# Router logits of two mixture-of-experts layers: gate columns as weights, tokens moving in two column halves

## The reference, cut to what matters

```python
# layer 0, x_flat: 625 x 1024, gate_w: 1024 x 8
router_logits = x_flat @ gate_w
router_probs = jax.nn.softmax(router_logits, axis=-1)
top_k_probs, top_k_idx = jax.lax.top_k(router_probs, 2)
...
# layer 1, xt: 625 x 1024, gate_w: 16 x 1024
scores = jax.nn.softmax((xt @ gate_w.T).astype(jnp.float32), axis=-1)
top_w, top_i = jax.lax.top_k(scores, 2)
```

## Time and profile of the kernel before

| | us |
|---|---|
| median of 3 runs | 1849.68 (1846.18 to 1851.08) |
| the profiled execution | 1855.41 |
| its span, first to last instruction | 1853.6 |
| PE busy in it | 1773.3 (96%) |
| DVE, ACT, POOL busy | 743.3, 404.6, 644.7 |
| mean granted PE clock | 0.976 |

### The profile page before, as it was taken

One profiled execution on the slowest core, in us unless ns is written; L12 is line 12 of the kernel. 1 busy time (PEld: TensorE's weight loads), 2 busy tenths in 40 slices (PEclk: granted clock), 3 DMA queues, 4 the chain that ended last, 5 costly groups with the idle time before them and its releaser, 6 DMA issues. The chain is left out here.

```text
span 1853.6 us, 21767 instructions
## 1 busy us (share of the span) xinstructions
PE 1773.3 (96%) x8374; PEld 1118.6 (60%) x8374; DVE 743.3 (40%) x1528; ACT 404.6 (22%) x744; POOL 644.7 (35%) x539
## 2 busy tenths in 40 slices
PE   9999999998999999999999999999999999999963
PEld 5475446444545777556677765577654776676641
DVE  5885003233525222454355557530621222222227
ACT  1000000002411011001576757411000322222223
POOL 0657872120000186777888620000300222222220
PEclk9999999998999999999899999999999999999987
DMA  9663124271620144333222136060411799999943
GB/s 352 185 180 83 2 47 114 64 226 27 268 84 5 37 127 130 97 97 85 54 56 54 41 86 176 33 254 12 138 63 46 295 413 409 406 410 407 404 165 109
DMA packets 104468, 289.08 MB, mean 156 GB/s; under 512 B 61942, under 2 KB 69336, under 8 KB 91611
## 3 DMA queue, kind: packets, MB, share of 16 engines
q1 hardware_dynamic: 29033, 224.83, 32.7%
q0 software_dynamic: 68160, 51.85, 12.5%
q10 hardware_dynamic: 7198, 11.36, 2.0%
HBM read 257.19 MB, written 30.32 MB: 155 GB/s over the span
## 5 line engine op out<-in xcount | busy, mean ns | idle before, releaser
L609 POOL DMA_INDIRECT table_d<-wring x85 | 173.7, 2044 | 108.6 <-issue 68.9
L381 PE MATMUL bank<-wring,region_a 128*125 128x512 f32 x480 | 207.6, 593 | 1.6 <-DVE region_a L755 0.7
L972 POOL DMA_INDIRECT wring<-xl_d,wring x85 | 108.9, 1282 | 257.8 <-DMA xr_d<-flat_b 231.9
L381 PEld LDWEIGHTS bank<-wring,region_a 128*125 128x125 f32 x480 | 89.6, 188 | 115.3 <-issue 113.9
L2292 PEld LDWEIGHTS bank<-picked_t,wring 128*128 128x128 f32 x1280 | 145.3, 194 | 7.6 <-issue 7.3
L2292 PE MATMUL bank<-picked_t,wring 128*128 128x128 f32 x1280 | 147.2, 278 | 0.1
L397 PE MATMUL bank<-flat_d,wring 128*128 128x312 f32 (+1 forms) x512 | 135.0, 426 | 0.0
L985 POOL DMA_INDIRECT score_d<-wring x85 | 110.7, 1302 | 68.3 <-DMA score_d<-wring 46.1
L972 POOL DMA_INDIRECT wring<-xr_d,wring x85 | 111.1, 1307 | 25.9 <-issue 24.4
L397 PEld LDWEIGHTS bank<-flat_d,wring 128*128 128x128 f32 x512 | 96.7, 189 | 37.9
L2307 PE MATMUL bank<-wring,unit_t 128*128 128x512 f32 x160 | 74.0, 605 | 0.0
(11 more groups left out here) (432 smaller groups left out, 2740.0 us busy)
## 6 DMA issues: line engine op xcount, KB each, us to landing
wring<-in_experts SPq DMA_DIRECT2D x60, 2048.0 KB, 12.8
wring<-in_L_Ws SPq DMA_DIRECT2D x6, 2048.0 KB, 27.0
table_d<-eq_buf SPq DMA_DIRECT2D x2, 3072.0 KB, 28.2
score_d<-no_edge SPq DMA_DIRECT2D x2, 3072.0 KB, 32.5
wring<-table_d POOLq DMA_DIRECT2D x10, 610.4 KB, 7.3
wring<-score_d SPq DMA_DIRECT2D x5, 1093.8 KB
wring<-pid_d ACTq DMA_DIRECT2D x17, 312.5 KB, 4.1
wring<-in_edge_w ACTq DMA_DIRECT2D x17, 312.5 KB, 5.2
```

What stands on the lines that cost most here:

```text
L381: ins = pe.matmul(bank[0:R, :], act_t[:, k, tok(t)], w[:, k * HALF:(k + 1) * HALF], start=(k == 0), stop=(k == chunks - 1))
L609: pool.indirect_dma_start(out=tables_d[b % 2], out_offset=bass.IndirectOffsetOnAxis(ap=edge_at[:, b:b + 1], axis=0), in_=edge_sums[:, b, : ...
L972: pool.indirect_dma_start(out=to[:, g % 2, j, :], out_offset=None, in_=table, in_offset=bass.IndirectOffsetOnAxis(ap=index[:, b:b + 1], ax ...
```

## The change

The roles of the two operands are exchanged. The gate columns become the weights (128 partitions by 64 columns, SMALL = 64) and the turned tokens move through them. Of the five tiles the even ones (0, 2, 4: 375 columns) give partitions 0 to 63 of the bank, the odd ones (1, 3: 250 columns) give partitions 64 to 127; the two alternate within each chunk, 16 matmuls for a router. The result has the gate columns on the partitions, so it is turned back: DVE copies both halves from PSUM to SBUF (`dve_keep_logits`; in layer 0 to new room in a weight slot, in layer 1 to `hid_sq`, which is free then), and PE makes three transposes into a second `dring` bank (`pe_turn_logits`). In layer 0 they stand after the fourth of the eight matmuls of half 0, tile 3; in layer 1 behind the first piece of L1932. In layer 1 PE now waits for all five turned tiles before the first matmul. `dve_top2` reads the second bank, with rows 64 columns apart.

```diff
-        def pe_logits(pe, act_t, gate, ne, before=None):
+        def pe_logits(pe, act_t, gate, ne):
             bank = dring.produce(pe)
-            for t in range(T):
-                if before:
-                    before(t)
-                for k in range(K):
-                    ins = pe.matmul(bank[0:R, t * GATE_W:(t + 1) * GATE_W], act_t[:, k, tok(t)],
-                                    gate[:, k * ne:k * ne + GATE_W], start=(k == 0), stop=(k == K - 1))
+            for k in range(K):
+                tiles = act_t[:, k, :].rearrange("p (t r) -> p t r", r=R)
+                for odd in range(2):
+                    ins = pe.matmul(bank[odd * SMALL:(odd + 1) * SMALL, 0:(T + 1 - odd) // 2 * R],
+                                    gate[:, k * ne:k * ne + SMALL], tiles[:, odd:T:2, :],
+                                    start=(k == 0), stop=(k == K - 1))
             ins.then_inc(d_filled, 1)
+            return dring.made, dring.produce(pe)
+
+        def pe_turn_logits(pe, made, bank, flat):
+            pe.wait_ge(d_emptied, made)
+            for t in range(0, T, 2):
+                rows = P if t < T - 1 else SMALL
+                ins = pe.transpose(bank[0:R, t * SMALL:t * SMALL + rows], flat[0:rows, t // 2 * R:(t // 2 + 1) * R],
+                                   ident[0:rows, 0:rows])
+            ins.then_inc(d_filled, 1)
+
+        def dve_keep_logits(v, flat):
+            bank = dring.consume(v)
+            for odd in range(2):
+                rows, n = slice(odd * SMALL, (odd + 1) * SMALL), (T + 1 - odd) // 2 * R
+                ins = v.tensor_copy(flat[rows, 0:n], bank[rows, 0:n])
+            ins.then_inc(d_emptied, 1)
...
                         for k in range(K):
+                            if (h, t, k) == (0, 3, K // 2):
+                                pe_turn_logits(pe, *flat_logits, flat0)
                             ins = pe.matmul(bank[0:R, :], x_t[:, k, tok(t)], w[:, k * HALF:(k + 1) * HALF],
                                             start=(k == 0), stop=(k == K - 1))
...
-                            pe_logits(pe, x_t, gate8, NE0)
+                            flat_logits = pe_logits(pe, x_t, gate8, NE0)
...
                 v.wait_ge(rank_made, 1)
+                dve_keep_logits(v, flat0)
                 dve_top2(v, router, NE0, 1)
...
-                pe_logits(pe, x3_t, gate16, NE1, before=lambda t: pe_wait_turned(pe, turned[t]))
+                for t in range(T):
+                    pe_wait_turned(pe, turned[t])
+                flat_logits = pe_logits(pe, x3_t, gate16, NE1)
...
+                        if m == 0 and at == 0:
+                            pe_turn_logits(pe, *flat_logits, hid_sq)
...
+                dve_keep_logits(v, hid_sq)
                 v.wait_ge(ffn_consts.sem, 7)
                 v.wait_ge(rank_made, 2)
                 dve_top2(v, r1, NE1, 2)
```

More of the change, by code:

```diff
@@ L861, in gps_kernel @@
         router = Router(spare, None, "r0", NE0)
+        flat0 = spare("flat0", [P, 3 * R])
         assert spare_at[0] <= 4096
@@ L888, in per_row @@
                 return x.unsqueeze(2).to_broadcast([R, T, ne])
-            bank = dring.consume(v)[0:R, 0:T * GATE_W].rearrange("r (t e) -> r t e", e=GATE_W)[:, :, 0:ne]
+            bank = dring.consume(v)[0:R, 0:T * SMALL].rearrange("r (t e) -> r t e", e=SMALL)[:, :, 0:ne]
             step(v.tensor_reduce(r.top[:, 0, :], bank, AX.X, ALU.max))
```

## The result

| | before | after |
|---|---|---|
| median of 8 runs, us | 1850.38 | 1843.10 |
| lowest, highest without the one stray run of before (6207.8), us | 1846.18, 1854.91 | 1840.62, 1848.25 |
| ratio, 95% interval | | 0.9968 (0.9953 to 0.9982) |
| span of the profiled execution, us | 1853.6 | 1839.3 |

The change makes the kernel about 0.3% faster: 5.9 us by the ratio, with 3.3 to 8.7 as its interval. The forecast was 1844.6 and 5.1 us.

A forecast was written before the change was run, and what follows sets the result against it. The prediction took PE, busy for 96% of the span, to bound the kernel. Gains of 3.1 us in layer 0 and 2.05 in layer 1 sum to 5.1, from 1849.68 to 1844.6 us, with a range of 1841.5 to 1851.5.

The forecast's parts named there:

- Bound by PE, and the gain travels: Whole kernel: PE is busy 96% of the span, so time saved in the first router should reach the program's end.
- Rival (c): Downstream of layer 0: its gain is swallowed by something not moving with PE, leaving 2.05 us, 1847.6; chance 0.07.
- The sign named for (c): From layer 0's logits to layer 1's transposes L318: the distance shrinks by 3.1 us, or else the gain was swallowed.
- The pace: Both routers' logits: unequal halves overlap, the longer sets 0.315 us a record; 16 records 5.04 us, 5.24 with form changes.
- The two changes of form: Each router's logits: going into the halved form and out again costs 0.20 us.
- The transposes: Each router: three transposes cost 0.32 us plus 0.08 for the 64-row last one, together 0.40.
- the net of layer 0: Layer 0's router: 8.71 us removed, 5.24 and 0.40 added, 3.1 us less.
- The copies by DVE: Between logits and transposes: copies of both halves take 0.96 us, with 2.4 us of slack in layer 0, costing nothing.
- Layer 1: the start: Layer 1's logits wait for all five tiles: PE idles 1.0 us, a wait on DVE adds 0.05; gain 2.05 us.
- rival (a): Layer 1: the clock falls after the new 1.0 us gap, leaving a gain of 3.4 us, 1846.3; chance 0.22.
- My comparison by the length of a gap: Layer 1's idle 1.0 us: lies between a harmless 0.91 us gap and 1.20 followed by a fall, nearer the harmless.
- The sum: Whole kernel: 3.1 us from layer 0 plus 2.05 from layer 1, 5.1 us or 0.28%, median 1844.6.

The follow-up runs named there:

- the three measurements of the changed kernel: The changed kernel measured and then rerun twice without an edit, against the kernel before: ratios 0.9968, 0.9973 and 0.9962.
- the second profile of before: The kernel before, profiled again without an edit: stage 0 36.20 us, the middle stretch 667.29 us, stage 1 82.05 us.
- the third of after: The changed kernel run a third time without an edit, against the kernel before: ratio 0.9962 (0.9936 to 0.9989).
- the run with the piece first: Changed kernel with the shared expert's first piece put ahead of layer 1's logits: stage 1 79.74 us instead of 80.60; ratio to before 0.9966.

## Why the prediction was right, point by point

**Bound by PE, and the gain travels.** Right, as far as the scatter lets it be seen. The stretch behind stage 1 took 145.42 and 145.44 us in the two profiles of before and 143.71 to 146.73 in those with a change, the longest with the lowest granted clock (0.98). In the middle the mean of the profiles with the old layer 0 (673.65, 667.29, 668.18) is 669.7, that of the nine with a new one 668.5; with 9.5 us of scatter this alone could not exclude a loss of 2 us. Rival (c) falls by the times of the whole: the three measurements of the changed kernel gain at least 3.3, 1.7 and 2.0 us at the lower ends of their intervals, and stage 1 alone would give 1.5. The sign named for (c), the distance from the logits of layer 0 to L318 in layer 1, was no test: it shrank by 11.7 us and not by 3.1, and it is 703.49 in the second profile of before and 703.07 in the third of after.

**The pace.** Forecast 5.24 us per router with its changes of form, measured 5.22 and 5.19 (1207.77 to 1212.96) for the block alone. The overlap of unequal halves, which no row of before had shown, behaves as L2354 and L2299 did: the longer half sets it. The run with both in the same partitions, 8.58 us, shows what decides it.

**The two changes of form were undersized.** The term was 0.20 us for going into the halved form and out again. Measured in layer 0: 0.09 in the records ahead, 0.18 in the block above its 16 x 0.315, 0.10 in the eight records behind (3.54 for 3.44), together 0.37. In layer 1, where PE comes out of a wait, it is 0.15 and 0.11.

The Trainium skill's page "TensorEngine Tiling (Array Packing)", section "Tiling Modes", has a change of the tiling mode drain the TensorE. The traces agree that there is a price, and size it with these figures; that a drain is what costs it, no run shows.

**The transposes were undersized.** The term was 0.40 us: 0.32 for three and 0.08 for the small one. Measured: 0.56 for the three, and 0.08 in the 56 records behind (24.13 for 24.05), 0.64 in all. I had taken 0.08 between nothing and 0.20 for the odd form; at 128 rows it went away with 0.33 us, above my upper end. Both terms together make the net of layer 0 2.66 us (2.75 in the stage) and not 3.1.

**The copies by DVE** took 0.97 and 0.98 us for the pair (forecast 0.96) and were done 2.4 us ahead of the transposes (508.75 against 511.12), as forecast. They cost nothing. `dve_top2` starts 9.42 us behind the logits' start, before 8.98, and the `multiply_up` behind it comes 0.45 later in the same count (forecast 0.33 for both); the next one still waits 1.73 us for ACT, so the slip ends there.

**Layer 1: the start came later than forecast.** The logits began 5.96 us behind the first transposes before, and 7.29 after: 1.33 later and not 1.02. DVE's last copy ended at 1207.42 and PE started at 1207.77, 0.35 behind it, where I had 0.05 from another wait (DVE hid_t, L2086). What the 0.35 is made of no run shows; ahead of the full-width piece in the run with the piece first it is some 0.4. From the logits' start on the stage gave 2.79 us (76.10 before, 73.31 after) where the sum had 3.07. Together 2.05 - 0.31 - 0.28 = 1.46 us, as measured.

This compares a profile of before in which the clock fell during the transposes with one of after in which it did not. The old form in layer 1 without a fall (the run with layer 0 alone changed):

```profile
1201.38 3.60 PE L318 MATMUL bank<-ident,region_a 125*128 125x125 f32 x32 [2.60 <-PEq L1123]
1206.03 1.07 PE L318 MATMUL bank<-ident,region_a 125*128 125x125 f32 x8 [1.04 <-DVE region_a L357]
1206.94 8.88 PE L877 MATMUL bank<-gate,x_t 128*125 128x100 f32 x80
```

There the logits began 5.56 us behind the first transposes, and the stage took 81.66. The new form takes 80.60 to 80.63 with the fall and without it, since the copies set its start. So the gain of layer 1 is 1.4 to 1.5 us where the clock fell in both and 1.0 to 1.1 where it fell in neither.

**The clock, rival (a).** It did not fall. Behind the new gap in the profile after (us, PE busy, granted clock, DMA share, GB/s):

```profile
1206.47:1207.47 1.00, 0.00 (x0) 1.00 0.30 121
1207.47:1208.47 1.00, 0.70 (x7) 1.00 0.24 94
1208.47:1209.47 1.00, 1.00 (x11) 1.00 0.21 78
1209.47:1210.47 1.00, 1.00 (x10) 1.00 0.32 131
```

It stayed at full in all six other profiles with this gap, of 1.17 to 1.60 us. My comparison by the length of a gap was too simple: the wait of 1.20 us ahead of the experts' loop, which was followed by a fall in the earlier trace rows and made the first 128 records take 16.19 us, is there in all twelve profiles, and the records take 16.19 in three of them and 14.56 in the other nine, the second profile of before among these. Chain of work of that profile (1.20 us of waiting stand ahead of its first row):

```profile
1433.67 1.08 PE bank L2275 x8
1434.78 0.70 DVE picked_t L2379
1435.52 14.56 PE bank L2292 x128
```

**The sum.** 5.1 us forecast, 4.1 in the stages (2.66 + 1.46), 5.9 by the ratio with 3.3 to 8.7 as the interval. The mechanism was right, and three terms (the changes of form, the odd transpose, the start behind a wait) were too small by 1.0 us in all. That the time of the whole, 1843.10, comes out on the far side of 1844.6 is chance: the eight executions of the changed kernel lie between 1840.62 and 1848.25, and the fall of the clock in the experts' loop alone is worth 1.6 us.

## What to carry to other kernels

A product with few result columns was cheaper here with those columns as weights, split over groups of result partitions that run at once, not within the same partitions; the cost is then the longest group's columns, so balance the groups, and check that they really stand in different partitions. Try a transpose that comes amid full-width matmuls at full height, even if half of it is zeros: it saved 0.33 us per router here. When an edit turns waits tile by tile into one wait for all, put work that needs only the first tiles in front; and where single profiles differ by 10 us, compare the stretches that the edit touches before believing the span.

## What the runs showed that I had not expected

- The stretch of 670 us between the two layers' routers varies by 9.5 us (664.18 to 673.65) from one execution to the next, in kernels with and without the change, while the stages of one form repeat to 0.03 us at like clock. Part of it goes with the granted clock (0.98 in five profiles of 668.18 to 673.65 us, 0.99 in seven of 664.18 to 668.48); what sets the clock's falls is not settled. Waits of PE for DVE of 1.8 to 2.3 us in it come and go (they are in 7 of 12 profiles).
- After the same wait of 2.60 us ahead of the transposes of layer 1 the granted clock fell to 0.50 for some 3 us in seven of the twelve profiles, both of before among them, and stayed at 1.00 in five, among them the first profile of after. The old form's stage 1 took 82.06 with the fall and 81.66 without it, only 0.40 less, since the transposes then wait for DVE instead; the new form's took 80.60 to 80.63 either way.
- A transpose of 64 rows amid full-width work costs 0.33 us more than one of 128, 0.23 at its place and 0.10 in the records behind.
- Four groups of 32 partitions, with one set of weights loaded every 0.055 us, run as fast as the longest group allows: 3.50 us for 64 records. The old logits took 0.109 us a record, above the 0.083 of their 100 columns; what held them there was not tested.
